# Window attention and a sharpened 1x1 convolution on one core: the Laplacian moves from VectorE to ScalarE and GpSimd

## The reference

```python
def _L1_conv_ref(x, merge_w, merge_b):
    lap = jnp.array([[0.0, -1.0, 0.0], [-1.0, 4.0, -1.0], [0.0, -1.0, 0.0]], dtype=x.dtype)
    ...
    edges = lax.conv_general_dilated(x, lap_k, window_strides=(1, 1), padding=((1, 1), (1, 1)), ...)
    out = x + edges
    y = lax.conv_general_dilated(out, merge_w, window_strides=(1, 1), padding='VALID', ...)
    return y + merge_b[None, :, None, None]
...
x = x + _L0_conv_ref(_gn(x), ...)
x = x + _L1_conv_ref(_gn(x), L1_conv_merge_w, L1_conv_merge_b)
```

## Time and profile before

| | value |
|---|---|
| median of three executions | 6071.18 us |
| span of the profiled execution, first to last instruction | 6061.7 us |
| what lies around the span, against that median | 9.5 us |
| busy: TensorE, VectorE, ScalarE, GpSimd | 96%, 83%, 52%, 33% |
| attention part, to the end of block 127 | about 5830 us |
| last blocks without attention, from block 130 on | from 5877 us |

### The profile page before, as it was taken

The page is one execution under the profiler, slowest core; times in us unless marked ns, Lnnn a source line. Parts: engine busy times, 40 slices in busy tenths (PEclk is TensorE's granted clock), DMA queues, the critical chain, the costliest instruction groups (busy, mean ns, idle before and its releaser), DMA issues.

```text
span 6061.7 us, 210224 instructions
## 1 busy us (share of the span) xinstructions
PE 5826.5 (96%) x93708; PEld 5135.1 (85%) x93708; DVE 5059.8 (83%) x8287; ACT 3165.5 (52%) x6020; POOL 2011.1 (33%) x1286
## 2 busy tenths in 40 slices
PE   7999999999999999999999999999999999999987
PEld 5888888888888888888888888888888888888876
DVE  4777788888888888888888888888888888888876
ACT  2555555555555555555555555555555555555531
POOL 1333333333333333333333333333333333333310
PEclk9999999999999999999999999999999999999999
DMA  4221123323333233332333323332333322222235
GB/s 130 71 58 58 54 75 104 98 81 93 95 104 101 75 92 99 101 97 80 95 101 100 93 80 93 106 101 86 86 96 98 106 84 69 82 79 75 80 93 163
DMA packets 392599, 550.79 MB, mean 91 GB/s; under 512 B 24918, under 2 KB 284825, under 8 KB 391706
## 3 DMA queue, kind: packets, MB, share of 16 engines
q1 hardware_dynamic: 391708, 537.35, 30.9%
HBM read 335.93 MB, written 201.33 MB: 89 GB/s over the span
## 4 chain that ended last, share of the span: by engine, by line
PE 82%; DVE 8%; ACT 7%; issue 1%; DMA 1%; SPq 0%; DVEq 0%
PE b_q L481 22%; PE b_t L570 10%; PE b_s L587 7%; PE b_q L556 7%; PE b_t L546 6%; PE b_s L489 5%; PE b_s L486 5%; PE b_t L528 4%; PE b_s L432 3%; PE b_s L434 3%; PE b_t L518 3%; ACT qkh L940 2%; DVE qkl L874 2%; PE b_s L441 2%; PE b_s L443 2%; PE b_s L442 2%
## 5 line engine op out<-in xcount | busy, mean ns | idle before, releaser
L1047 POOL TENSOR_TENSOR probs<-probs,srec 128x768 f32<-128x768 f32 x512 | 880.7, 1720 | 2211.8 <-DVE srec L923 2211.8
L1036 POOL TENSOR_TENSOR probs<-probs,smax 128x768 f32<-128x768 f32 x512 | 754.1, 1473 | 1519.7 <-DVE smax L885 1519.7
L880 DVE TENSOR_TENSOR probs<-b_s,posb 128x768 f32<-128x768 f32 x512 | 488.3, 954 | 660.3 <-PE b_s L587 659.4
L940 ACT ACTIVATE vs<-b_q 128x192 f32<-128x192 f32 x1024 | 339.2, 331 | 1294.3 <-PE b_q L481 1294.3
L481 PE MATMUL b_q<-wnh,xh 128*128 128x288 f32 x2048 | 700.7, 342 | 67.0 <-DVE qkl L874 65.7
L874 DVE TENSOR_TENSOR qkl<-b_q,qkh 128x384 fp32r<-128x384 f32 x1024 | 566.5, 553 | 176.9 <-ACT qkh L940 139.7
L489 PEld LDWEIGHTS b_s<-yT,wp 128*128 128x128 f32 x4096 | 618.5, 191 | 52.3
L489 PE MATMUL b_s<-yT,wp 128*128 128x128 f32 x4096 | 622.4, 275 | 0.0
L486 PE MATMUL b_s<-yT,wp 128*128 128x256 f32 x2048 | 613.5, 381 | 1.5 <-DVE probs L880 0.9
L481 PE MATMUL b_q<-wnl,xhl 128*128 128x288 f32 x2048 | 606.5, 296 | 0.0
L481 PE MATMUL b_q<-wnh,xhb 128*128 128x288 f32 x2048 | 606.3, 296 | 0.0
(11 more groups left out here) (155 smaller groups left out, 13688.6 us busy)
## 6 DMA issues: line engine op xcount, KB each, us to landing
ld<-in_x SPq DMA_DIRECT2D x192, 512.0 KB, 4.6
late<-x_dram SPq DMA_DIRECT2D x112, 640.0 KB, 4.8
xs<-in_x SPq DMA_DIRECT2D x128, 512.0 KB, 5.4
x_dram<-late SPq DMA_DIRECT2D x128, 512.0 KB, 3.0
out<-late SPq DMA_DIRECT2D x128, 512.0 KB, 3.0
late<-x_dram SPq DMA_DIRECT2D x240, 192.0 KB, 5.4
xs<-in_x SPq DMA_DIRECT2D x128, 256.0 KB, 5.9
x_dram<-late SPq DMA_DIRECT2D x128, 256.0 KB, 3.7
```

The source lines that it names most:

```text
L880: V.tensor_tensor(scored(i).rearrange("p (t q) m -> p t q m", q=4), scores.rearrange("p (t q m) -> p t q m", q=4, m=N), posb[:, :, :].unsq ...
L940: return A.activation(o, i, ACT.Copy)
L1036: P.tensor_tensor(probs[:, i % 2, :, :], probs[:, i % 2, :, :], smax[:, i % 2, :].unsqueeze(2).broadcast_to([128, 12, N]), ALU.subtract).t ...
L1047: P.tensor_tensor(probs[:, i % 2, :, :], probs[:, i % 2, :, :], srec[:, i % 2, :].unsqueeze(2).broadcast_to([128, 12, N]), ALU.mult).then_ ...
```

## The change

The Laplacian is written as `z = 5 * centre` on ScalarE (`centre`), then on GpSimd `dg` as before (`diagonal`), `z = z - dg[0:4, 0:W]` and `z = z - dg[1:5, 1:W+1]` (`neighbours`, two halves). Nothing of it is left on VectorE. ScalarE's part stands behind the copy `osb`, in doubles 0, 1 and 2 of a block. GpSimd's part of a unit comes one double later: the diagonal and the first half ahead of the subtraction of the maximum, the second half ahead of the multiplication by the reciprocal. The border columns are written only for strips 0, 1 and 2 of an image, once for each of the three buffers.

```diff
+        border_count = list(itertools.accumulate(int(v % NS < 3 or v % NS == NS - 1) for v in range(STRIPS)))
...
+        units = ((src_a, 0, za, 0), (src_b, 0, zb, 0), (src_a, 4, za, 512))
+
+        def stencil_unit(j):
+
+            blk, ph = divmod(2 * j, 8)
+            v = blk - STENCIL_LAG
+            return (v, ph // 2) if 0 <= v < STRIPS and ph < 6 else None
...
 # VectorE
-            def diagonal(v, unit):
...
-            def neighbours(v, unit):
...
-            def stencil(v, unit):
...
             def border(v):
 
                 s = v % NS
-                for t, src in ((0, src_a), (1, src_b)):
+                if 3 <= s < NS - 1:
+                    return
+                if s < 3:
+                    for t, src in ((0, src_a), (1, src_b)):
...
-                edges(2 * j)
                 norms(2 * j)
                 if pair(0):
                     remainders(2 * j + 1)
-                edges(2 * j + 1)
...
 # ScalarE
+            def centre(v, unit):
+
+                src, r, zz = unit_views(v, unit)
+                if unit == 0:
+                    act.wait_ge(src_in[v % 3], 48 * (v // 3 + 1))
+                    if v >= 2:
+                        act.wait_ge(m_mm, m_count[8 * (v - 2 + MERGE_LAG) + PIECES - 1])
+                A.activation(zz, src[:, r + 1:r + 5, 1:W + 1], ACT.Copy, scale=5.0).then_inc(five_done, 1)
...
                     copy(osb[:, :, :].rearrange("p k n -> p (k n)"), o_out_ps).then_inc(o_out, 1)
+                if stencil_unit(j):
+                    centre(*stencil_unit(j))
                 if pair(0):
...
 # GpSimd
+            def diagonal(v, unit):
+
+                src, r, _ = unit_views(v, unit)
+                if unit == 0:
+                    pool.wait_ge(border_w, border_count[v])
+                    pool.wait_ge(src_in[v % 3], 48 * (v // 3 + 1))
+                pool.wait_ge(z_done, 3 * v + unit)
+                P.tensor_tensor(d, src[:, r + 1:r + 6, 0:W + 1], src[:, r:r + 5, 1:W + 2], ALU.add
+                                ).then_inc(diag_done, 1)
+
+            def neighbours(v, unit, half):
+
+                _, _, zz = unit_views(v, unit)
+                n = 3 * v + unit + 1
+                if half == 0:
+                    pool.wait_ge(diag_done, n)
+                    pool.wait_ge(five_done, n)
+                    P.tensor_tensor(zz, zz, d[:, 0:4, 0:W], ALU.subtract).then_inc(nb_done, 1)
+                else:
+                    pool.wait_ge(nb_done, n)
+                    P.tensor_tensor(zz, zz, d[:, 1:5, 1:W + 1], ALU.subtract).then_inc(z_done, 1)
+
             for j, pair in doubles():
+                unit = stencil_unit(j - 1)
+                if unit:
+                    diagonal(*unit)
+                    neighbours(*unit, 0)
                 if pair(2):
...
+                if unit:
+                    neighbours(*unit, 1)
                 if pair(2):
```

More of the change, by code:

```diff
@@ L1 @@
+import itertools
 from contextlib import ExitStack
@@ L194, in program @@
         sub_done, norm_done = map(sem, ("sub_done", "norm_done"))
-        border_w, diag_done, nb_done, z_done = map(sem, ("border_w", "diag_done", "nb_done", "z_done"))
+        border_w, five_done, diag_done, nb_done, z_done = map(sem, (
+            "border_w", "five_done", "diag_done", "nb_done", "z_done"))
         loads = [
@@ L246, in m_wait, with unit_views @@
                 eng.wait_ge(a_read, a_count[it])
+        units = ((src_a, 0, za, 0), (src_b, 0, zb, 0), (src_a, 4, za, 512))
[3 more added lines that the diff above has]
+            return (v, ph // 2) if 0 <= v < STRIPS and ph < 6 else None
+        def unit_views(v, unit):
+            src, r, z, at = units[unit]
+            return src[v % 3], r, z[:, v % 2, at:at + 512].rearrange("p (r c) -> p r c", c=W)
         def doubles():
@@ L708, in scored @@
                 return probs[:, j % 2, :, :]
-            units = ((src_a, 0, za, 0), (src_b, 0, zb, 0), (src_a, 4, za, 512))
-            def diagonal(v, unit):
[L714 to L720, removed]
-            def neighbours(v, unit):
[L724 to L728, removed]
-            def stencil(v, unit):
[L732 to L736, removed]
             def border(v):
                 s = v % NS
-                for t, src in ((0, src_a), (1, src_b)):
[L742 to L745, removed]
+                if 3 <= s < NS - 1:
+                    return
+                if s < 3:
+                    for t, src in ((0, src_a), (1, src_b)):
+                        tile = src[v % 3]
+                        count = (10, 6)[t]
+                        last = V.tensor_scalar(tile[:, :, 0:PW:PW - 1],
+                                               ones[:, 0:1].unsqueeze(2).broadcast_to([128, count, 2]),
+                                               sm[:, 2, t:t + 1], None, ALU.mult)
                 if s in (0, NS - 1):
@@ L795, in m_result @@
                     bias(at % 2, p, m_count[it])
[L797 to L816, removed]
             def borders(it):
@@ L1031, in _ @@
             P.memset(ones[:, :], 1.0).then_inc(ones_done, 1)
+            d = dg[:, :].rearrange("p (r c) -> p r c", c=W + 1)
+            def diagonal(v, unit):
[16 more added lines that the diff above has]
+                    P.tensor_tensor(zz, zz, d[:, 1:5, 1:W + 1], ALU.subtract).then_inc(z_done, 1)
             for j, pair in doubles():
+                unit = stencil_unit(j - 1)
+                if unit:
+                    diagonal(*unit)
+                    neighbours(*unit, 0)
                 if pair(2):
```

## The result

The changed kernel takes 6156.06 us in the median of four executions (6154.96 to 6158.33), the kernel before beside it 6071.32. The ratio is 1.0143, with a 95% interval from 1.0129 to 1.0158: slower by 85 us. The forecast was 6134 us.

The account below looks back on a forecast made before the run. TensorE, busy 96% of the span, was taken as the bound, with the Laplacian on the path in 16 last blocks. 6071 - 40 (attention part) + 103 (last blocks) = 6134 us; range 6074 to 6185.

Parts of the forecast that it names:

- The last blocks, the main term: Blocks from 130 on: a chain over ScalarE and GpSimd makes the period 17.2 us, 103 us more in all.
- Lower clock after the wait: Last blocks: TensorE idles 7 us and restarts at the lower clock, 17.2 us a block instead of 15.5.
- Rival 2: Last blocks at full clock: 15.5 us a block, +76 us, time 6107 us; chance 0.15.
- GpSimd's price: New GpSimd operations at L1042's price, 4.17 us a unit; 3.2 us, from L1036, as the lower end.
- its first two terms: Attention part: double 0 behind L744 gains 20 us, double 1 behind L758 gains 16 us.
- the 0.42 us of double 0: Blocks c = 5 to 12 of an image: held border operation L744 delays L880; 48 blocks, 20 us gained.
- the 0.17 of double 1: Double 1 of about 97 blocks: scores wait for VectorE's L758, 0.17 us each; 16 us gained.
- Blocks c = 13 and c = 2 ... I take zero: 12 blocks where a norm is made: gain and GpSimd pressure taken as zero, +23 and -30 us kept for the range.
- The 9.5 us around the span: Whole kernel: the profiled execution's time taken as its span plus some 9.5 us, that is, the median 6071.2 us.
- Rival 4: No difference: 14 to 14.5 us a last block against 50 us won, 6065 to 6080 us; chance 0.07.
- Rival 1: Image boundaries: GpSimd pressure delays VectorE, 2.5 us in 12 blocks, 30 us, time 6164 us; chance 0.2.
- the small chain, L614 to L616: Boundary blocks: small VectorE operations could wait for GpSimd's diagonal and first half, 2.5 us before L880.

Follow-up runs that it names:

- The two border runs: Kernel before with border columns for strips 0, 1 and 2 only: 6049.00 us, 0.9963; changed kernel with border columns for every strip: 6160.47 us, 1.0149.
- the first run: Changed kernel, but from block 130 on VectorE does the Laplacian as in the kernel before: 6055.83 us, ratio 0.9984.
- the second of them: Changed kernel with last blocks' Laplacian on VectorE and GpSimd's diagonal and first half behind the subtraction in blocks c = 13 and c = 2: 6012.70 us, 0.9905.

## Why the prediction was right, and which of its steps were off

- **The last blocks, the main term: right, and for the reason given.** 17.2 us a block forecast, 17.08 measured; +103 forecast, +101.7 measured. That the number fits so closely is partly luck, for two of its parts were off and cancelled. GpSimd's unit was forecast at 4.17 us from L1042 and is 1.55 + 1.18 + 1.18 = 3.91. Piece 1's result was forecast to end 5.05 us after piece 0's start, and it ends at 5955.71 + 0.47 - 5950.65 = 5.53.
- **Lower clock after the wait: right.** The run with TensorE kept busy puts it at 2.25 us a block.
- **Rival 2, full clock:** didn't happen; the same run shows what it would have given, 14.8 us a block rather than 15.5, since GpSimd is cheaper.
- **GpSimd's price:** between my two ends. The Trainium skill (GPSIMD Engine Reference, Performance versus the Vector engine) gave an estimate of 1.12 and 1.42 us; the trace has 1.18 and 1.55.
- **Ordinary blocks: the size was right, the reason half.** The sum of its first two terms was 36 us; the blocks of these kinds gave 40. But I put the 0.42 us of double 0 down to the border edit, and only the 0.17 of double 1 to the Laplacian. The two border runs show that either alone removes the 0.42 us, that only the Laplacian removes the 0.17, and that with the Laplacian gone the border's part is worth nothing that can be measured.
- **The step that failed: "Blocks c = 13 and c = 2 ... I take zero".** They cost 28.8 us more than before, the low end that I kept for the range. So the attention part won 12 us instead of 40. In spans the forecast was 28.6 us short (63 against 91.6): 27.7 from the attention part, 2.2 from the end, less 1.3 from the last blocks. In medians it is only 22, because of the next point. That the time fell into the range is due to its width.
- **The 9.5 us around the span** were not that: by the 1.8 us that other executions have around theirs, the profiled one was simply quicker than the median. In differences of medians it does no harm; differences of spans against this profile come out 7 us too large.
- **Rival 4's sum** was off: 14 to 14.5 us a block against 50 us won is 6073 to 6081 us, not 6065 to 6080.
- **Rival 1 was the mechanism, in the wrong main place.** I priced the small chain, L614 to L616, at up to 2.5 us a block; there it held L631 and L633 and cost a 1.40 us wait. The larger part was in the next double, where GpSimd's diagonal and first half hold the casts of the weights (2.79 us of waiting, with the clock down behind it). I had seen such a cast at 1.2 us in the trace before and not asked what would run beside the others. The right place and the wrong one are told apart by the runs with GpSimd's operations moved behind: 23 us come from double 2 of c = 13 alone, and against the first run, which has the same last blocks, the second of them takes 33.1 us less in the blocks c = 13 and 12.0 in c = 2. So the pressure cost 45 us, not 30, and what the boundaries win without it is 15 us, not 23.

The Trainium skill (SBUF — State Buffer, Who interferes with whom) says that `cast` and `tensor_scalar` in a two-port mode, and operations with two SBUF inputs while GpSimd's reads SBUF, wait out a GpSimd operation that started first. The rows agree for the casts (0.44 against 1.83 us) and for two elements (0.16 against 1.48).

## What to carry to other kernels

Work moved off an engine that doesn't bound the kernel gains only where the bounding engine waits for it, so find those waits first and price them one by one; then look for the stage where the moved work is the bound itself, here 16 blocks of 147 that cost more than all the others won. Where GpSimd gets new work, list VectorE's operations that will run beside it, the small ones and the casts too, and put GpSimd's operations where TensorE doesn't wait for what they hold: moved behind the subtraction, they held another operation (2.12 us instead of 0.74) at a cost of 0.28 us. A chain over two engines pays for the program order as well as for the work: the centre stood behind a result that it didn't need, and with the order turned round 55 of the 102 us were gone.

## What the runs showed of the hardware that was not expected

- A VectorE operation of 64x576 elements takes 0.44 us alone and 1.83 beside GpSimd's diagonal. Beside each other, VectorE's 0.69 us sum takes 1.93 and GpSimd's 1.55 us diagonal 2.22, so that sharing elementwise work between the two saved nothing: the stretch of the last blocks is 168.6 us with one unit on GpSimd and 168.6 with all on VectorE.
- GpSimd's two-input operation takes 1.18 us for 512 elements in rows of 128, and 1.55 us for 645 in rows of 129, while the existing one of 768 elements with a repeated input takes 1.47.
- Useless matmuls during a wait made a kernel some 30 us faster (6125.85 against 6156.06 us; 1.0097 against 1.0143 of the kernel before), by holding TensorE at its higher clock (granted clock 1.00 over the last blocks instead of 0.80).
